# Part of every eighth unit's tanh moved to GpSimd and VectorE in a fused Flamingo block

## The reference

```python
txt_proj = jnp.einsum('btd,de->bte', textual_features, Ws)
feat_proj = jnp.einsum('bfd,de->bfe', features, W)
h = jnp.tanh(txt_proj[:, None, :, :] + feat_proj[:, :, None, :] + b)   # [B, F=1024, T=64, D=512]
rho = jnp.einsum('bftd,d->bft', h, w[:, 0])
rho = rho + (1.0 - qm)[:, None, :] * NEG
att = jax.nn.softmax(rho, axis=-1)
txt_h = jnp.einsum('bft,btd->bfd', att, textual_features)
w_s = jnp.tanh(jnp.einsum('bfd,od->bfo', txt_h, Wcw) + bcw)            # Wcw, Wcb: [1, D]
b_s = jnp.tanh(jnp.einsum('bfd,od->bfo', txt_h, Wcb) + bcb)
x = x + tanh(g) * (w_s * features + b_s)                               # features = layernorm(x)
```

## Time and profile before

| | |
|---|---|
| median of 3 runs | 1926.75 us (1923.69 to 1926.92) |
| profiled execution, its own time | 1925.59 us |
| its span, first to last instruction | 1923.5 us |
| tanh of the 244 full units | 87.2 us to 948.7 us of the span |
| granted TensorE clock, mean | 0.985 |

### The profile page before, as it was taken

How to read it: one execution, slowest core, us unless ns; L and a number is a source line. 1 busy time by engine, 2 the same in 40 slices (tenths; PEclk the granted TensorE clock), 3 DMA queues, 4 the chain that set the end, 5 groups by cost and what they waited for, 6 DMA issues and landing times.

```text
span 1923.5 us, 24394 instructions
## 1 busy us (share of the span) xinstructions
PE 1577.8 (82%) x9406; PEld 708.5 (37%) x9473; DVE 1713.1 (89%) x2626; ACT 1476.9 (77%) x1091; POOL 613.9 (32%) x482
## 2 busy tenths in 40 slices
PE   7778965688556975786489978999999987899996
PEld 4232211122111321232134435666666653444442
DVE  6999999999999998889689977899999867999997
ACT  4899999999999999999745755445554436888881
POOL 1000000000000000000044236666666643999991
PEclk9999999999999999999989989999999999999999
DMA  5000200010000010000079884333333111122212
GB/s 205 2 7 19 85 12 1 22 65 30 6 1 0 18 36 25 1 1 12 0 249 395 289 243 138 102 112 110 115 102 109 44 55 39 44 78 77 66 55 77
DMA packets 123269, 146.54 MB, mean 76 GB/s; under 512 B 31374, under 2 KB 80654, under 8 KB 122770
## 3 DMA queue, kind: packets, MB, share of 16 engines
q1 hardware_dynamic: 123154, 144.98, 23.0%
HBM read 87.55 MB, written 51.77 MB: 72 GB/s over the span
## 4 chain that ended last, share of the span: by engine, by line
ACT 44%; PE 30%; DVE 14%; issue 4%; POOL 4%; DMA 3%; SPq 1%; DVEq 0%; ACTq 0%; POOLq 0%
ACT unit L557 41%; PE psum L1762 5%; PE psum L1796 5%; PE psum L1058 4%; PE psum L1748 3%; DVE unit L463 2%; POOL h L1937 2%; PE psum L1772 2%; PE psum L1789 2%; PE psum L1819 2%; DVE psum L1528 1%; DVE psum L1533 1%; POOL hidden L1954 1%; PE psum L1781 1%; PE psum L609 1%
## 5 line engine op out<-in xcount | busy, mean ns | idle before, releaser
L557 ACT ACTIVATE unit<-unit 128x4096 f32<-128x4096 f32 x244 | 857.4, 3606 | 0.5 <-DVE unit L463 0.3
L463 DVE TENSOR_SCALAR unit<-feat_proj,text_proj 128x1024 f32<-128x1024 f32 x976 | 667.5, 746 | 64.4 <-PE psum L697 61.5
L697 PE MATMUL psum<-unit,w_pad 128*32 128x512 f32 x3904 | 470.4, 600 | 227.9 <-ACT unit L557 227.7
L697 PEld LDWEIGHTS psum<-unit,w_pad 128*32 128x32 f32 x3904 | 102.0, 109 | 543.2 <-ACT unit L557 386.9
L744 POOL TENSOR_SCALAR red<-red 128x8 f32<-128x8 f32 x4 | 2.0, 508 | 531.5 <-DVE red L338 531.5
L1819 PE MATMUL psum<-xq_block,w_q 128*128 128x512 bf16 x489 | 119.9, 385 | 15.7 <-ACT h L1695 11.2
L1937 POOL TENSOR_TENSOR h<-h,arow 128x512 f32<-128x512 f32 x104 | 125.6, 1231 | 20.0 <-ACT h L1695 20.0
L744 POOL TENSOR_SCALAR rstd<-mv 128x8 f32<-128x8 f32 (+1 forms) x5 | 1.7, 335 | 406.1 <-DVE mv L233 406.1
L609 PE MATMUL psum<-xnT,W_sb 128*128 128x512 f32 x256 | 125.5, 619 | 1.9 <-ACT xnT L511 1.9
L1670 ACT ACTIVATE scores<-scores 128x1024 f32<-128x1024 f32 x32 | 33.9, 1058 | 114.0 <-POOL scores L1923 114.0
L1954 POOL TENSOR_TENSOR hidden<-hidden,srow 128x2048 f32<-128x2048 f32 x28 | 114.4, 4084 | 10.1 <-DVE hidden_q L1563 9.7
(11 more groups left out here) (260 smaller groups left out, 2695.7 us busy)
## 6 DMA issues: line engine op xcount, KB each, us to landing
h_scratch<-h SPq DMA_DIRECT2D x44, 512.0 KB, 6.1
hin<-h_scratch SPq DMA_DIRECT2D x32, 704.0 KB, 4.6
xin<-in_x SPq DMA_DIRECT2D x8, 1024.0 KB, 5.6
tern_in<-in_w1T SPq DMA_DIRECT2D x16, 512.0 KB, 6.0
tern_in<-in_w2T SPq DMA_DIRECT2D x16, 512.0 KB, 6.9
x<-in_x SPq DMA_DIRECT2D x16, 512.0 KB, 3.7
x_scratch<-x SPq DMA_DIRECT2D x32, 256.0 KB, 2.0
x3in<-x_scratch SPq DMA_DIRECT2D x31, 256.0 KB, 3.2
```

What stands on the lines that cost most here:

```text
L463: ins = ve.tensor_scalar(units[:, n % 3, k, :], FP[:, bi % 2, k, :], TP[:, k, n:n + 1], None, ALU.add)
L557: ac.activation(units[:, n % 3], units[:, n % 3], ACT.Tanh).then_inc(unit_tanh, 1)
L697: mm = te.matmul(psum[k * TG:(k + 1) * TG, 3 + 2 * grp + half, :], w_pad[:, k, TG - 1 - tt:2 * TG - 1 - tt], units[:, n % 3, k, half * BAN ...
```

## The change

In 26 of the 244 full units (n mod 32 = 1, 9, 17, 25 in the first group of a batch, 1, 9, 17 in the second; the first batch begins at 17) the last eighth, chunk 3 of the second half (128 x 512 elements), is not summed by VectorE nor passed through ScalarE's tanh. It is computed as 1 - 2 / (1 + exp(2(f + t))). The exponential is a product of two: f and t are each split into a whole number of steps of ln2 / 2 (as a float's exponent bits) and a remainder; exp of the remainders is taken once a batch.

- once a batch, GpSimd: five instructions of `split` (two on 128 x 512, three on 128 x 64); VectorE: four of `remainder`; ScalarE: two exponentials, 128 x 512 and 128 x 64 (`mantissas`)
- each of the 26 units, GpSimd: three instructions on 128 x 512 (`light_denominator`: exponents added and limited, times the feature mantissa, times the text mantissa plus 1); VectorE: two reciprocals on 128 x 256, two and three units later (`reciprocals`); TensorE: one matmul on 128 x 512 with -2w in place of one of the eight, four units later (`light_sum`); once a group one matmul that adds w for the 1 of the formula
- ScalarE's tanh of such a unit is on 128 x 3584, and the fourth addition of VectorE on 128 x 512
- `tail`: the mask is put into PSUM by a matmul of one row (`rho_mask`) and the strips are summed onto it, so VectorE's addition of the mask goes; the product with cb_row moves to GpSimd (`products`); of the last batch the first half of rho is copied as soon as the first half of the last unit is multiplied, and the second by ScalarE
- GpSimd's roots take their turn at fixed units in its new loop over all units

`pool_chunks` is 0 for every unit, so GpSimd's loop over chunks adds nothing. The core of the diff:

```diff
+    LIGHT_FIRST, LIGHT_END, LIGHT_EVERY = 1, (28, 24), 8
+    LIGHT = [bi * TXT + grp * TG + tt for bi in range(NB) for grp in range(2)
+             for tt in range(LIGHT_FIRST + (16 if bi + grp == 0 else 0), LIGHT_END[grp], LIGHT_EVERY)]
+    REC_AFTER, SUM_AFTER = (2, 3), 4
+    SPLIT_AT, REST_AT = 60, (62, 63)
...
-            if s == 11:
+            if s == 13:
                 V.wait_ge(sel_mm, 4 * bi + 4)
-                ve.tensor_tensor(rho[:, :, :], psum[:, 7, :].rearrange("p (f t) -> p f t", t=TXT),
-                                 text_row(neg_row, bi), ALU.add).then_inc(tail_step, 1)
...
+        def remainder(bi, step):
+            if step == 0:
+                V.wait_ge(light_step, split_count(bi) + 5)
+                for out, exp, val in ((feat_mant[:, :], feat_exp[:, :], feat),
+                                      (text_mant[:, :], text_exp[:, 0, :], TP[:, KC - 1, cols])):
+                    ve.scalar_tensor_tensor(out=out, in0=exp, scalar=-HALF_LN2 / EXPONENT, in1=val, op0=ALU.mult,
+                                            op1=ALU.add).then_inc(light_vec, 1)
...
+        def reciprocals(n):
+            for part, after in enumerate(REC_AFTER):
+                if n - after in LIGHT:
+                    j = LIGHT.index(n - after)
+                    piece = light[:, j % 2, part * (BANK // 2):(part + 1) * (BANK // 2)]
+                    V.wait_ge(light_step, light_count(n - after) + 3)
+                    ve.reciprocal(piece, piece).then_inc(light_vec, 1)
...
+        for step in range(2):
+            remainder(0, step)
         for n in range(RAMP, NU):
...
-            for k in range(KC):
-                ins = ve.tensor_scalar(units[:, n % 3, k, :], FP[:, bi % 2, k, :], TP[:, k, n:n + 1], None, ALU.add)
+            for k in range(pool_chunks(n), KC):
+                part = slice(0, BANK * (light_half(n) if k == KC - 1 else 2))
+                ins = ve.tensor_scalar(units[:, n % 3, k, part], FP[:, bi % 2, k, part], TP[:, k, n:n + 1], None, ALU.add)
             ins.then_inc(unit_added, 1)
+            reciprocals(n)
+            if t in REST_AT and bi + 1 < NB:
+                remainder(bi + 1, REST_AT.index(t))
...
-            ac.activation(units[:, n % 3], units[:, n % 3], ACT.Tanh).then_inc(unit_tanh, 1)
+            unit = units[:, n % 3].rearrange("p k s -> p (k s)")[:, 0:(2 * KC - 2 + light_half(n)) * BANK]
+            ac.activation(unit, unit, ACT.Tanh).then_inc(unit_tanh, 1)
+            if n == RAMP:
+                mantissas(0)
+            if t == TXT - 1 and bi + 1 < NB:
+                mantissas(bi + 1)
+        A.wait_ge(unit_mm, NU - RAMP)
+        A.wait_ge(sel_mm, 4 * NB - 2)
+        ac.activation(RP[:, 1, :], psum[:, 6, :], ACT.Copy).then_inc(ramp_tanh, 1)
...
+        def rho_mask(bi):
+            T.wait_ge(tail_step, (bi - 1) * TAIL_STEPS + RHO_SUB)
+            te.matmul(psum[:, 7, :].rearrange("p (f t) -> p f t", t=TXT), ones[0:1, :],
+                      neg_row[0:1, bi * TXT:(bi + 1) * TXT].unsqueeze(1).broadcast_to([1, TPB, TXT]), start=True, stop=False)
...
+        def light_denominator(n):
+            G.wait_ge(light_mm, j - 1)
+            gp.tensor_scalar(den.bitcast(U32), feat_exp[:, :], text_exp[:, 1, t:t + 1], TOP, ALU.add,
+                             ALU.min).then_inc(light_step, 1)
+            gp.tensor_tensor(den, den, feat_mant[:, :], ALU.mult).then_inc(light_step, 1)
+            gp.tensor_scalar(den, den, text_mant[:, t:t + 1], 1.0, ALU.mult, ALU.add).then_inc(light_step, 1)
...
+        for n in range(RAMP, NU):
+            bi, t = divmod(n, TXT)
+            G.wait_ge(fp_copied, (bi + 1) * 2 * KC)
+            G.wait_ge(unit_mm, n - 2 - RAMP)
+            if n in LIGHT:
+                light_denominator(n)
+            if t == 20 and bi > 0:
+                products(bi - 1)
+            if t == SPLIT_AT and bi + 1 < NB:
+                split(bi + 1)
```

More of the change, by code:

```diff
@@ L8 @@
 I32 = mybir.dt.int32
+U32 = mybir.dt.uint32
 U8 = mybir.dt.uint8
@@ L309, in tail @@
                 ve.reciprocal(red[:, 2, :], red[:, 1, :]).then_inc(tail_step, 1)
[L310 to L317, removed]
+            if s == 21:
+                V.wait_ge(text_copied, TEXT_DONE)
+                V.wait_ge(tail_step, done + ATT_INV)
+                ve.tensor_tensor(prod[:, 0], att[:, :, :], text_row(cw_row, bi), ALU.mult).then_inc(tail_step, 1)
+            if s == 23:
+                V.wait_ge(tail_step, done + PROD_W)
+                ve.tensor_reduce(red[:, 3, :], prod[:, 0], AX.X, ALU.add).then_inc(tail_step, 1)
+            if s == 27:
+                V.wait_ge(prod_b_done, PROD_B0 + bi + 1)
+                ve.tensor_reduce(red[:, 4, :], prod[:, 1], AX.X, ALU.add).then_inc(tail_step, 1)
             if s == 29:
@@ L651, in ramp_rho, with light_sum @@
             mm.then_inc(ramp_mm, 1)
+        def light_sum(n):
+            bi, t = divmod(n, TXT)
+            grp, tt = divmod(t, TG)
+            strip = slice((KC - 1) * TG, KC * TG)
+            if tt == CONST_AT or n == RAMP:
+                T.wait_ge(start_step, 3)
+                te.matmul(psum[strip, 4 + 2 * grp, :], w_light[:, 0 if bi + grp == 0 else 2 - grp, :],
+                          ones[:, 0:1].broadcast_to([P, BANK]), start=False, stop=False,
+                          tile_position=(0, (KC - 1) * TG))
+            if n - SUM_AFTER in LIGHT:
+                j = LIGHT.index(n - SUM_AFTER)
+                at = (n - SUM_AFTER) % TG
+                T.wait_ge(light_vec, reciprocal_count(n - SUM_AFTER) + 2)
+                te.matmul(psum[strip, 4 + 2 * grp, :], w_neg[:, TG - 1 - at:2 * TG - 1 - at], light[:, j % 2, :],
+                          start=False, stop=False, tile_position=(0, (KC - 1) * TG)).then_inc(light_mm, 1)
         def keys(m, k0, k1):
@@ L695, in tensor_A @@
             for half in range(2):
-                for k in range(KC):
+                for k in range(KC - half * (2 - light_half(n))):
                     mm = te.matmul(psum[k * TG:(k + 1) * TG, 3 + 2 * grp + half, :],
@@ L750, in gpsimd_A @@
             root(mv[:, q * TPK:(q + 1) * TPK, 1], rstd0[:, q * TPK:(q + 1) * TPK], TPK, rstd0_done, TPK)
[L751 to L760, removed]
+        moments_root(1)
+        split(0)
+        for n in range(RAMP, NU):
+            bi, t = divmod(n, TXT)
+            G.wait_ge(fp_copied, (bi + 1) * 2 * KC)
+            G.wait_ge(unit_mm, n - 2 - RAMP)
+            G.wait_ge(text_copied, KC if bi == 0 else 2 * KC)
+            if n < RAMP + 3:
+                G.wait_ge(ramp_mm, 2 * (RAMP - SLOTS // 2 + n - RAMP + 1))
+            for k in range(pool_chunks(n)):
+                gp.tensor_scalar(units[:, n % 3, k, :], FP[:, bi % 2, k, :], TP[:, k, n:n + 1], None, ALU.add)
+            if n in LIGHT:
+                light_denominator(n)
+            if t == 10 and 0 < bi < NB - 1:
+                moments_root(bi + 1)
+            if t == 20 and bi > 0:
+                products(bi - 1)
+            if t == 40 and bi > 0:
+                gate_root(bi - 1)
+            if t == SPLIT_AT and bi + 1 < NB:
+                split(bi + 1)
+        products(NB - 1)
+        gate_root(NB - 1)
     def sync_A():
```

125 lines of the change are left out of this document (109 added, 16 removed).

## The result

The changed kernel takes 2001.68 us (median of 5 runs, 1996.17 to 2003.95) against 1924.17 us (5 runs): a ratio of 1.0391 (interval 1.0378 to 1.0405), 77.5 us slower. The forecast was slower, at 1988 us (+61 us), with its own range 1970 to 2003 us and the range 1935 to 2015 us. It was added to the median of the first three executions before, 1926.75 us; two more executions brought that median to 1924.17 us. So the time is 13.7 us above the forecast and the slowdown 16.5 us.

What follows compares the result with a forecast made beforehand. ScalarE bounds the kernel, VectorE a very close second that becomes the bound. Terms 57.2 + 5.3 + 1.0 - 2.4 = +61 us on the 1926.75 us median gave 1988 us; own range 1970 to 2003, wider range 1935 to 2015.

Steps and rivals of the forecast that it cites:

- The reciprocal: VectorE, two on 128x256 in each light unit: 1.68 us each, bounds 0.48 and 2.07 us.
- B: Rival: reciprocals cheap at 0.48 us, GpSimd collides with VectorE's additions; 1935 us, chance 0.08.
- C: Rival: cheap reciprocals and little collision, so ScalarE stays the bound; 1917 us, chance 0.13.
- D: Rival: reciprocals at 7.5 ns a column (+19 us) or collision for GpSimd's full length (+28 us); 2007 or 2016 us, chance 0.09.
- The collision: VectorE's additions held up beside GpSimd's three instructions: 1.4 us a light unit, bounds 0 and 2.55 us.
- Rival A: Reciprocals are dear, but GpSimd hardly collides with VectorE; 1948 us, chance 0.17.
- Units 16 to 191: First stretch, 19 light units: VectorE needs 678.5 us and sets the end, +57.2 us.
- Units 192 to 247: Last batch's stretches, VectorE's sum against ScalarE's: +0.8 and +4.5 us, together +5.3 us.
- Start: Before unit 16: remainder (1.7 us) and collision with split (about 1 us) meet a 1.7 us lead, +1.0 us.
- Behind the last unit: Mask addition and one product leave VectorE, first half copied earlier, second copy on ScalarE: -2.4 us.
- Stages B and C: The stages after stage A: no change in length, 0 us.
- The signs named beforehand: Changed profile: light tanh 3.18 us, additions stretched to 1.1 to 1.8 us only in light units, last batch's period near 3.5 us.

Runs made afterwards that it cites:

- every sixteenth unit: Changed kernel with a light unit in sixteen units in place of eight, 15 in place of 26: 1966.07 us, 1.0214 of the kernel before.
- the last batch alone: Changed kernel with five light units, all in the last batch, and GpSimd's work beside the reciprocals: 1934.13 us, 1.0046 of the kernel before.
- the pair of halves and quarters: Four light units, last batch only; each one's reciprocals in two halves (1928.82 us) or four quarters with a later matmul (1924.33 us).

## Why the prediction was right, point by point

The time lies inside the forecast's own range, 1.3 us from its upper end, and the mechanism is the forecast one; one term of the sum was too small.

- **VectorE takes over as the bound.** Right: 99% busy in units 16 to 191, the chain changes engine, and doubling the reciprocals costs their full length.
- **The reciprocal, 1.68 us by a line through four small shapes.** Measured 1.742 us for 256 columns. The line was good although it was carried from 16 columns to 256. The cheap reciprocal of rivals B and C is out, and so is the 2.07 us of D. The estimate from the Trainium skill ("VectorE: DVE Perf Modes", section "First, the fixed hardware budget"), a repeat count of 8 read as 8 cycles a column, 2.28 us, is 0.54 us too long: the measurement decides, with 6.3 ns a column.
- **The collision, 1.4 us a light unit.** Split and products included, it was forecast at 26 x 1.4 + 5.7 = 42 us. Against the kernel before, with 26 additions at 477 ns (a mean of 739 ns), it is (784 - 739) x 976 = 44 us; the three instructions alone are 46 us by the run that shortens them. The two counts differ by more than split and products, so either is good to some us only. Rival A (no collision) is out by the run with short GpSimd instructions (33 us), and rival D's full length as well. The route to it was partly wrong, and that the total came out is in part luck: GpSimd's first instruction was priced at 0.64 us and lasts 2.2 to 6.9 us, but beside unit 49 it holds up two of four additions and not one: the second by 0.44 us (the first three take 2.52 us in place of 2.08 us) and the fourth, of 512 columns, by 0.35 us (0.82 us in place of 0.48). That is twice the estimate of 0.38 us. The third addition runs at its usual speed while GpSimd's instruction is still under way (227.71 to 230.44 us, above):
```profile
227.47 2.52 DVE L542 TENSOR_SCALAR unit<-feat_proj,text_proj 128x1024 f32<-128x1024 f32 x3
...
229.90 0.82 DVE L542 TENSOR_SCALAR unit<-feat_proj,text_proj 128x512 f32<-128x512 f32 x1
```
The Trainium skill's rule ("SBUF — State Buffer", section "Who interferes with whom") that GpSimd holds the port pair it shares with VectorE for the whole instruction does not agree with this instruction's trace.
- **Units 16 to 191, +57.2 us.** Measured +61.1 us. VectorE's busy time was forecast at 678.5 us and is 674.5 us; 7.4 us of idle time that the sum did not have come on top. Part of this agreement is luck: reciprocals and collisions were each a little dearer than forecast, and the busy time came out 4 us lower all the same; why was not looked into.
- **Units 192 to 247, +5.3 us: the mis-sized term.** Measured +14.1 us. The sum set VectorE's whole spare time of 141 us against all its added work. The spare time lies where there is no lateness: VectorE idles there for 6.5 us while ScalarE idles for 8.1 us. The runs with every sixteenth unit (expected 1944 to 1954, measured 1966 us), with the last batch alone (1934 us where the sum gave 1921 to 1924) and the pair of halves and quarters showed the mechanism. Of the 16 us by which the slowdown passed the forecast, 4 + 9 us are in these two stretches, and 5.7 us in stages B and C; the other parts take 2 us off.
- **Start, +1.0 us.** Nothing: the additions of unit 16 start at 97.0 us in both profiles. That the lead absorbed it is likely and not shown: in the runs that have the same start, unit 16 starts at 96.4 to 98.7 us, so 1 us cannot be told here.
- **Behind the last unit, -2.4 us.** Measured -2.1 us in the profile.
- **Stages B and C, 0.** 5.7 us longer in the changed kernel's profile (962.4 us from the reciprocal of q_scale to the end, 956.7 us before). The profiles of the ten experiments have 956 to 961 us for this part, and those that keep every light unit with all its work have 956.5 us (doubled reciprocals) and 957.7 us (GpSimd beside the reciprocals), so it does not come with the change; what it is stays open. It was one execution, and the changed kernel's runs scatter by 8 us.
- **The signs named beforehand.** The light tanh has 3.18 us, as said. The stretched additions are not only in light units: as much of the stretching can fall into the unit behind (units 49 and 50 above). The last batch's period is not near 3.5 us but 149.6 / 40 = 3.74 us, which is the mis-sized term again.

## What to carry to other kernels

Before work is moved to the second-busiest engine, price it against that engine's spare time per unit of the pipeline, not per stretch: with three buffers, here, spare time could not be carried over more than about 2 us. Work put on GpSimd is not free for VectorE's SBUF-to-SBUF instructions; 46 us of collision fell to 18 us by starting it beside instructions that do not collide (reciprocals). A part worth 0.43 us to ScalarE that costs VectorE 2 x 1.66 - 0.27 + 1.77 (46 us of collision over 26 units) = 4.8 us needs that engine to be idle, in that place, for as long.

## What the runs showed of the hardware that had not been expected

- A VectorE reciprocal costs 190 ns for 8 columns, 941 ns for 128 and 1742 ns for 256 (f32, SBUF): (1742 - 941) / 128 = 6.26 ns a column, some twelve times an addition's 0.53 ns. The group of the quarters kernel:
```profile
L457 DVE RECIPROCAL light<-light 128x128 f32<-128x128 f32 x16 | 15.1, 941 | 0.0
```
- GpSimd's two-step instructions on 128x512 take very different times, and VectorE's additions lengthen them. Groups of the changed kernel: subtract and multiply 2.26 us, multiply and add 0.89 us in the mean; and L909 above, add and minimum written as uint32, 3.24 us in the mean.
```profile
L896 POOL TENSOR_SCALAR feat_exp<-feat_exp 128x512 f32<-128x512 f32 x4 | 9.0, 2256 | 0.3
...
L894 POOL TENSOR_SCALAR feat_exp<-feat_proj 128x512 f32<-128x512 f32 x4 | 3.6, 890 | 107.4 <-DVE feat_proj L325 107.0 <-DVE feat_proj L511 0.4
```
- The collision costs GpSimd as well. The shortest, median and longest L909 in the changed kernel, and the same instruction in the kernel that starts it beside the reciprocals:
```profile
L909 POOL TENSOR_SCALAR light<-feat_exp,text_exp x26: 2207/2732/6904, 100.7 to 963.0; 128x512 uint32<-128x512 f32 x26
```
```profile
L912 POOL TENSOR_SCALAR light<-feat_exp,text_exp x26: 1994/2416/3240, 102.4 to 924.1; 128x512 uint32<-128x512 f32 x26
```
The third instruction (multiply and add) falls from a median of 1.01 us to 0.70 us between the two kernels.
- GpSimd can be held up for long. In three of the 26 light units L909 lasts 6.8 to 6.9 us, each time over eight additions that follow each other without a gap and are not lengthened themselves. One of them:
```profile
377.23 6.83 POOL L909 TENSOR_SCALAR light<-feat_exp,text_exp 128x512 uint32<-128x512 f32 x1 [20.24 <-PE psum L817]
```
```profile
378.48 5.12 DVE L542 TENSOR_SCALAR unit<-feat_proj,text_proj 128x1024 f32<-128x1024 f32 x8
```
- The granted TensorE clock in units 16 to 191 is 0.97 in place of 1.00, with TensorE busy 74% of the time (75% before): it fell from 2.4 to 1.2 GHz in some short stretches. One of them, between two at full clock (the third number from the end is the clock):
```profile
212.00:215.50 3.50, 1.52 (x16) 0.58 (x12) 3.50 (x7) 2.35 (x1) 0.00 (x0) 1.00 0.00 0
215.60:218.90 3.30, 3.30 (x17) 0.93 (x10) 3.30 (x6) 1.73 (x1) 0.00 (x0) 0.50 0.76 269
219.00:222.50 3.50, 3.27 (x20) 0.91 (x19) 3.50 (x8) 3.50 (x2) 0.00 (x0) 1.00 0.30 115
```
What that costs is within VectorE's 7.4 us of idle time there; it was not separated.
